# y through memory in rows by channel, and the tail one batch ahead inside the up projections

## The reference, cut to what matters

```python
# x: (4, 512, 256); 32 heads of width 8, state 64; everything in fp32
sa, ca, ga, sb, cb, gb = modulation(c)                      # per batch, per channel
h = layernorm(x) * (1 + ca) + sa
proj = h @ W_in.T                                           # xBC | z | A_log
xBC = causal_conv4(xBC) + conv_b                            # per channel, 4 taps
xh, Bm, Cm = split(xBC)                                     # (l, 32, 8), (l, 32, 64), (l, 32, 64)
a = -softplus(A_log);  Lm = exp(segsum(a))                  # lower triangle of decays, per head
M = einsum('blhn,bshn,bhls->bhls', Cm, Bm, Lm)
y = einsum('bhls,bshp->blhp', M, xh) + D * xh
x = x + ga * (y * silu(z + z_bias) @ W_out.T)
h = layernorm(x) * (1 + cb) + sb
x = x + gb * (fwht(silu(h @ W1.T) * (h @ W3.T)) @ W2.T)     # hidden width 1024
```

## Time and profile before

| | |
|---|---|
| median of 3 runs | 618.3 us |
| the profiled execution's own time | 619.35 us |
| its span | 617.5 us |
| PE busy | 591.9 us, 96% |
| DVE busy | 474.5 us, 77% |
| ACT busy | 382.0 us, 62% |
| POOL busy | 222.9 us, 36% |
| chain that ended last | PE 89%, DVE 7%, issue 2%, ACT 1%, POOL 1% |
| DMA | 51.75 MB, mean 84 GB/s |

### The profile page before, as it was taken

One profiled execution on the slowest core, in us unless ns is written; L12 is line 12 of the kernel. 1 busy time (PEld: TensorE's weight loads), 2 busy tenths in 40 slices (PEclk: granted clock), 3 DMA queues, 4 the chain that ended last, 5 costly groups with the idle time before them and its releaser, 6 DMA issues.

```text
span 617.5 us, 18850 instructions
## 1 busy us (share of the span) xinstructions
PE 591.9 (96%) x6890; PEld 488.6 (79%) x6890; DVE 474.5 (77%) x794; ACT 382.0 (62%) x953; POOL 222.9 (36%) x435
## 2 busy tenths in 40 slices
PE   3898999999999999999999999999969999999997
PEld 3787777877878887887887887887858898888987
DVE  4883989999999999989989989989575564455353
ACT  0665778778778868868868878877523404314240
POOL 2560257455455455346356356586010010000000
PEclk9997999999999999999999999999999999999999
DMA  8400533333332332342342342532020010010101
GB/s 295 196 0 4 194 130 102 102 110 97 96 114 89 98 119 85 100 121 80 100 126 74 99 133 69 170 100 76 32 68 1 0 55 15 0 34 1 35 0 35
DMA packets 29286, 51.75 MB, mean 84 GB/s; under 512 B 3268, under 2 KB 10052, under 8 KB 29000
## 3 DMA queue, kind: packets, MB, share of 16 engines
q1 hardware_dynamic: 29256, 51.34, 26.1%
HBM read 48.97 MB, written 2.37 MB: 83 GB/s over the span
## 4 chain that ended last, share of the span: by engine, by line
PE 89%; DVE 7%; issue 2%; ACT 1%; POOL 1%; DMA 0%; SPq 0%; DVEq 0%
PE ps L250 19%; PE ps L251 17%; PE ps L252 17%; PE ps L390 10%; PE ps L433 5%; PE ps L409 4%; PE ps L373 4%; PE ps L424 4%; PE ps L551 2%; PE ps L443 2%; DVE acc L889 2%; DVE acc L961 1%; DVE xn L867 1%; PE ps L261 1%; PE ps L453 1%
## 5 line engine op out<-in xcount | busy, mean ns | idle before, releaser
L961 DVE SCALAR_TENSOR_TENSOR acc<-ps,cw_dve,acc 128x510 f32<-128x510 f32 (+2 forms) x384 | 264.1, 740 | 32.6 <-ACT acc L688 31.2
L717 ACT ACTIVATE decay<-sums,p_slot 128x128 f32<-128x128 f32 x512 | 163.0, 394 | 1.1 <-POOL sums L1235 1.1
L1235 POOL TENSOR_SCALAR_AFFINE_SELECT sums<-sums 128x512 f32<-128x512 f32 x128 | 81.1, 635 | 183.3 <-DMA sums<-running_sums 182.7
L688 ACT ACTIVATE acc<-ps,cw_act 128x512 f32<-128x512 f32 x128 | 99.2, 775 | 48.5 <-PE ps L252 48.5
L250 PE MATMUL ps<-ht_hi,wg_hi 128*128 128x512 f32 x256 | 108.4, 424 | 0.0
L251 PE MATMUL ps<-ht_lo,wg_hi 128*128 128x512 f32 x256 | 101.7, 397 | 0.0
L252 PE MATMUL ps<-ht_hi,wg_lo 128*128 128x512 f32 x256 | 101.6, 397 | 0.0
L949 DVE TENSOR_TENSOR mix<-ps,decay 128x1024 f32<-128x1024 f32 x64 | 77.7, 1215 | 2.7 <-PE ps L390 2.7
L390 PE MATMUL ps<-acc 64*64 64x64 f32 (+1 forms) x2048 | 69.8, 255 | 1.0 <-DVE mix L949 1.0
L815 ACT ACTIVATE silu_sb<-ps 128x512 f32<-128x512 f32 x32 | 19.1, 598 | 72.4 <-PE ps L252 72.4
L390 PEld LDWEIGHTS ps<-acc 64*64 64x64 f32 x2048 | 54.4, 132 | 12.0 <-issue 12.0
(11 more groups left out here) (137 smaller groups left out, 975.7 us busy)
## 6 DMA issues: line engine op xcount, KB each, us to landing
sums<-running_sums SPq DMA_DIRECT2D x128, 256.0 KB, 3.2
wg_raw<-in_w_bc SPq DMA_DIRECT2D x8, 512.0 KB, 4.6
u_sb<-in_u SPq DMA_DIRECT2D x4, 512.0 KB, 8.2
stage<-in_w SPq DMA_DIRECT2D x1, 2048.0 KB, 12.2
u<-in_u SPq DMA_DIRECT2D x4, 512.0 KB, 3.4
out<-x_tok SPq DMA_DIRECT2D x3, 512.0 KB, 2.9
wmod_sb<-in_wmod SPq DMA_DIRECT2D x1, 1024.0 KB, 8.5
gates<-gate_rows SPq DMA_DIRECT2D x4, 256.0 KB, 3.5
```

Source lines behind the costliest of these rows:

```text
L688: af(acc[:, b % 2, t, :], ps[:, PROJ_BANK[t], :], ACT.Identity, bias=cw_act[:, t, 1:2], scale=cw_act[:, t, 0:1]).then_inc(s[f"tap_a{t}"], 1)
L717: i = af(decay[:, j, c * P:(c + 1) * P], sums[:, j, c * P:(c + 1) * P], ACT.Exp, scale=-1.0, bias=p_slot[:, b * CH + c, j:j + 1])
L961: stt(a[:, d:], ps[:, PROJ_BANK[t], 0:L - d], cw_dve[:, t, TAPS - 1 - d:TAPS - d], a[:, d:], ALU.mult, ALU.add).then_inc(s[f"taps{t}"], 1)
L1235: gp.affine_select(out=v, in_=v, compare_op=ALU.is_ge, fill=FAR, base=0, pattern=[[0, CH], [1, P]], channel_multiplier=-1).then_inc(s["mas ...
```

## The change

What it does:

- The y transposes of the head loop, the scaling by decays and the addition of D x in it, and the transposes of y in the tail are gone. ScalarE copies y of a unit (two buffers), and SyncE stores it to memory, by channel. The convolved x is stored by channel at the start, and so are the decay rows exp(-sum).
- For each batch of the tail SyncE loads (`load_front`) the inner y, the earlier y, the decay rows and x, all by channel, in 8 transfers. GpSimd combines y from its two parts (`y_sum`), VectorE adds D x and multiplies by silu(z) (`gate`).
- The order of a head step is new on every engine; scores of head pair 1 move into the next step, ahead of the other projections. Tiles are taken in the order 1, 0, 3, 2.
- In the tail the front of batch b+1 is inside the up projections of batch b: z projection ahead of tile 2, output projection ahead of tile 4, and on VectorE gate, residual, statistics and normalisation ahead of the products of tiles 3, 5, 6 and 7. The tail is written out for each batch instead of looped.

The diff, cut to its core:

```diff
+ORDER = (1, 0, 3, 2)
+PLACE = [ORDER.index(t) for t in range(GT)]
...
 # SyncE
+            for b in range(B):
+                for t in range(KT):
+                    n = KT * b + t
+                    sp.wait_ge(s["xtaps"], 3 * (n + 1))
+                    sp.dma_start(x_d[n * P:(n + 1) * P, :], acc[:, n // GT, n % GT, :]).then_inc(s[f"st_x{n // GT}"], 16)
...
+            def store_y(g, b):
+                sp.wait_ge(s["yt_ev"], g * B + b + 1)
+                sp.dma_start(y_d[bass.ds((b * NG + g) * P, P), :], yt_sb[:, b % 2, :]).then_inc(s["st_y"], 16)
+            def step(g, b, gr):
+                for j in range(3):
+                    load_sum(g, b, j)
+                if gr is not None:
+                    store_y(gr, (b - 2) % B)
+                load_sum(g, b, 3)
+            def load_front(b):
+                for kt in range(KT):
+                    own = y_d[(b * NG + 4 * kt) * P:(b * NG + 4 * kt + 4) * P, :].rearrange("(q r) l -> q r l", r=QD)
+                    load(yi[:, kt, :], own[:, 0:HD, :], "ld_front")
+                    load(yo[:, kt, :], own[:, HD:2 * HD, :], "ld_front")
+                    rows = e_d[b * NH + 16 * kt:b * NH + 16 * (kt + 1), :].unsqueeze(1).to_broadcast([16, HD, L])
+                    load(ee[:, kt, :], rows, "ld_front")
+                    load(xt[:, kt, :], x_d[(KT * b + kt) * P:(KT * b + kt + 1) * P, :], "ld_front")
...
+            sp.wait_ge(s["bfly"], 6)
+            sp.wait_ge(s["st_e"], 16 * CH)
+            sp.wait_ge(s["w_split"], NG * 2 * GT)
+            load_front(0)
+            store_y(NG - 1, B - 2)
+            sp.wait_ge(s["proj2"], NG * B)
+            load(u2[:], u_b[0], "ld_res")
+            store_y(NG - 1, B - 1)
+            sp.wait_ge(s["st_y"], 16 * NG * B)
+            for b in range(1, B):
+                sp.wait_ge(s["oproj"], 2 * b)
+                load_front(b)
+                sp.wait_ge(s["x1_done"], 2 * b)
                 load(u2[:], u_b[b], "ld_res")
...
 # TensorE
-                    pe.wait_ge(s["w_split"], (g * GT + t) * 2 + 2)
+                    pe.wait_ge(s["w_split"], (g * GT + PLACE[t]) * 2 + 2)
...
             def step(g, b, gq, gr):
+                proj(g, b, 1)
                 if r is not None:
                     states(r, br)
-                    proj(g, b, 0)
-                    proj(g, b, 1)
+                    scores(r, br, 1, False)
+                b_transposes(q, bq, 0, first)
+                proj(g, b, 0)
+                proj(g, b, 3)
+                proj(g, b, 2)
                 if r is not None:
                     inter(r, br, isinstance(r, int) and r == 0)
                     intra(r, br)
-                b_transposes(q, bq, 0, first)
                 scores(q, bq, 0, first)
-                    proj(g, b, 2)
-                    proj(g, b, 3)
                 b_transposes(q, bq, 1, first)
-                if r is not None:
-                    y_transposes(r)
-                scores(q, bq, 1, first)
...
+                    if b + 1 < B:                      # in up(b), per tile m
+                        if m == 2:
+                            z_project(b + 1, 4)
+                        if m == 4:
+                            pe.wait_ge(s["h32b_done"], KT * (b + 1))
+                            out_project(b + 1, 6)
...
+            z_project(0, 0)
+            states(q, B - 2)
+            scores(q, B - 2, 1, False)
+            b_transposes(last, B - 1, 0, False)
+            inter(q, B - 2, False)
+            intra(q, B - 2)
+            pe.wait_ge(s["bfly"], 6)
+            w2_transform(0)
+            w2_transform(1)
+            scores(last, B - 1, 0, False)
+            b_transposes(last, B - 1, 1, False)
+            out_project(0, 0)
+            scores(last, B - 1, 1, False)
+            states(last, B - 1)
+            w2_transform(2)
+            w2_transform(3)
+            inter(last, B - 1, False)
+            intra(last, B - 1)
+            norm2_transposes(0)
+            for b in range(B):
+                up(b)
+                down(b, 0)
+                down(b, 1)
+                if b + 1 < B:
                     norm2_transposes(b + 1)
                 down(b, 2)
                 down(b, 3)
...
 # ScalarE
             def last_tap(g, b, t):
+                if not (isinstance(n, int) and n < 2):
+                    if t == 1:
+                        act.wait_ge(s["score"], 8 * (n - 1))
+                    elif t:
+                        act.wait_ge(s["intra"], JH * (n - 1))
...
                 if r is not None:
                     state_copies(r)
                 decays(q, bq, 0, first)
                 decays(q, bq, 1, first)
+                last_tap(g, b, 1)
+                last_tap(g, b, 0)
+                decays(q, bq, 2, first)
+                b_evacuate(q, 0)
+                last_tap(g, b, 3)
+                last_tap(g, b, 2)
                 if r is not None:
+                    y_evacuate(r, b % 2, early=(isinstance(r, int) and r < 2))
+                b_evacuate(q, 1)
                 decays(q, bq, 3, first)
...
 # VectorE
+                tap(g, b, 1, 0)
                 tap(g, b, 0, 0)
+                tap(g, b, 1, 1)
                 tap(g, b, 0, 1)
+                tap(g, b, 1, 2)
+                tap(g, b, 0, 2)
                 mix_pair(q, 0, first)
+                tap(g, b, 3, 0)
                 tap(g, b, 2, 0)
+                tap(g, b, 3, 1)
                 tap(g, b, 2, 1)
+                tap(g, b, 3, 2)
                 mix_pair(q, 1, first)
                 tap(g, b, 2, 2)
...
             def gate(b):
+                dve.wait_ge(s["ysum"], b + 1)
                 for kt in range(KT):
+                    stt(yi[:, kt, :], xt[:, kt, :], d_ch[:, kt:kt + 1], yi[:, kt, :], ALU.mult,
+                        ALU.add).then_inc(s["y_x"], 1)
+                for kt in range(KT):
+                    dve.wait_ge(s["y_x"], KT * b + kt + 1)
                     dve.wait_ge(s["silu_z"], KT * b + kt + 1)
+                    tt(yi[:, kt, :], yi[:, kt, :], sz[:, kt, :], ALU.mult).then_inc(s["gated"], 1)
...
+                    if b + 1 < B:                      # in hidden(b), ahead of tile m
+                        if m == 3:
+                            gate(b + 1)
+                        if m == 5:
+                            residual1(b + 1)
+                        if m == 6:
+                            statistics2(b + 1)
+                        if m == 7:
+                            normalise2(b + 1)
...
+            w2_lower(0)
+            w2_lower(1)
+            mix_pair(last, 0, False)
+            gate(0)
+            residual1(0)
+            mix_pair(last, 1, False)
+            statistics2(0)
+            w2_lower(2)
+            w2_lower(3)
+            normalise2(0)
+            h2_low(0)
...
 # GpSimd
+                mask(n, 0)
                 if split:
                     await_unit("ld_wg", (g + 2) * 16)
+                    split_after(g, b, 1)
+                mask(n, 1)
+                if split:
                     split_after(g, b, 0)
                 scale_by_decays(g, n, b, early)
+                mask(n, 2)
                 own_x(g, n, b, early)
                 mask(n, 3)
                 if split:
+                    split_after(g, b, 3)
                     split_after(g, b, 2)
...
+            def y_sum(b):
+                pool.wait_ge(s["ld_front"], 16 * 8 * (b + 1))
+                for kt in range(KT):
+                    gp.tensor_tensor(yo[:, kt, :], yo[:, kt, :], ee[:, kt, :], ALU.mult).then_inc(s["y_scaled"], 1)
+                for kt in range(KT):
+                    pool.wait_ge(s["y_scaled"], KT * b + kt + 1)
+                    i = gp.tensor_tensor(yi[:, kt, :], yi[:, kt, :], yo[:, kt, :], ALU.add)
+                i.then_inc(s["ysum"], 1)
+            for b in range(B):
+                y_sum(b)
                 inverse_root(b, "eps2", "rs2")
```

More of the change, by code:

```diff
@@ L371, in b_transposes @@
                     pe.wait_ge(s["bt_ev"], 2 * q + p)
+                if not first and p == 0:
+                    pe.wait_ge(s["st_copy"], 2 * q)
                 for c in range(CH - 1):
@@ L588, in down @@
                 i.then_inc(s["down_mm"], 1)
-            def ffn_step(b, normed, ahead):
-                up(b, b + 2 if normed else B)
-                if normed:
-                    norm2_transposes(b + 1)
-                if ahead:
-                    z_project(b + 2, 0)
-                    z_project(b + 2, 1)
-                down(b, 0)
-                if ahead:
-                    yT_transposes(b + 2, 2)
-                down(b, 1)
-                if ahead:
-                    out_project(b + 2, 2)
+            last, q = NG * B - 1, NG * B - 2
@@ L790, in _ @@
                     step(g, b, gq=(g - 1 if b == 0 else g), gr=(g - 1 if b < 2 else g))
-            step(None, 0, gq=NG - 1, gr=NG - 1)
+            last, r = NG * B - 1, NG * B - 2
             def silu_gate(b):
@@ L813, in hidden @@
```

(5 more changed lines are left out.)

434 lines of the change are left out of this document (140 added, 294 removed).

## The result

The changed kernel takes **667.6 us** (median of 4, 665.8 to 667.8) against 618.1 us before (median of 4 on the same chip): ratio 1.079, 95% interval 1.077 to 1.081. The forecast was 638 us in a range of 618 to 656. The sign was right, and the time is 29.6 us above it. The profiled execution took 667.57 us, with a span of 665.8 us and a mean granted clock of 0.949.

What follows compares the result with a forecast made beforehand. TensorE, busy 54.00 of 54.00 us in the head loop, was taken as the bound. Span: 617.5 - 17.3 - 4.3 + 3.4 + 16.1 + 7.7 + 1.6 + 1.1 + 10.2 + 1.2 = 637.2, adjusted to 638 us; range 618 to 656.

Steps and rivals of the forecast that it cites:

- What TensorE no longer does: Head loop and tail: y transposes go, -17.3 and -4.3 us; rearranged steps of 11.3 us give back +3.4 us.
- The group boundary: Every fourth head step, 7 times: TensorE waits 2.3 us for GpSimd's split of tile 3, +16.1 us.
- The front of batch 0: Ahead of the first output projection: uncovered hole of 7.7 us for loads (7.5 us for eight), sum and gate.
- Inside the up projections: Tail, three batches: holes of 2.0 us at the output projection and 1.8 us at down(b, 0), +10.2 us net.
- The contention: Tail: normalisation on VectorE slowed beside GpSimd's sum of y, +1.2 us for two batches.
- The clock: TensorE's granted clock falls once, behind the hole ahead of the first output projection, +1.6 us.
- the clock falls at each wait: Rival, chance 0.13: TensorE's clock falls behind each hole, thirteen times 1.6 us, giving 659 us.
- The beginning: Start of the kernel: new stores and small loads on SyncE, ends -1 and +2 us, taken as 0.

Runs made afterwards that it cites:

- Experiment 2: Changed kernel with GpSimd's split of tiles 3 and 2 moved ahead of the fourth mask: 643.3 us.
- experiment 3: Changed kernel with GpSimd's sum of y for batches 1 to 3 waiting for the previous batch's normalisation: 661.8 us.
- experiment 4: Changed kernel with eight overwritten matmuls on TensorE ahead of the third tile's weight wait at each of seven group boundaries: 664.2 us.
- experiment 7: Kernel of experiment 2 with tail output projections one tile later, normalisation behind the last remainder, and GpSimd's sums waiting for the normalisation before: 618.5 us.
- experiment 8: Kernel of experiment 2 with overwritten matmuls put into TensorE's holes of the tail: 635.6 us.
- Experiment 5: Kernel of experiment 2 with the decay rows in their own buffer and without ScalarE's wait for their stores: 639.7 us.
- experiment 1: Changed kernel with the decay rows in their own buffer and without ScalarE's wait for their stores: 662.4 us.

## Why the prediction was too low

**What TensorE no longer does.** Right in sign, and worth more than forecast. The step was taken at 11.3 us with 11.19 as the lower bound and is 11.12. Three transposes behind the scores cost 0.31 us (260.77 to 261.08), less than the 0.48 of the earlier trace rows: the bound took the dear place of a neighbour for granted. In the loop that is -18.3 us for a forecast of -13.9.

**The group boundary.** Right: 16.1 forecast, 17.5 measured, with the place and the releaser as named. The walk on the earlier trace rows can be checked link by link on the timelines after (ScalarE's fourth decays; GpSimd's mask, cast and `wg_lo`; TensorE's third tile):

```profile
344.08 1.29 ACT L725 ACTIVATE decay<-sums,p_slot 128x128 f32<-128x128 f32 x4
...
348.86 0.63 POOL L1190 TENSOR_SCALAR_AFFINE_SELECT sums<-sums 128x512 f32<-128x512 f32 x1 [3.87 <-DMA sums<-running_sums]
349.44 0.40 POOL L1138 CAST wg_hi<-wg_raw 128x256 fp32r<-128x256 f32 x1
350.03 0.72 POOL L1140 TENSOR_TENSOR wg_lo<-wg_raw,wg_hi 128x256 fp32r<-128x256 f32 x1 [0.19 <-POOL wg_hi L1138]
...
350.81 0.50 PE L296 MATMUL ps<-ht_hi,wg_hi 128*128 128x512 f32 x1 [2.46 <-POOL wg_lo L1140]
```

Experiment 2 removes it by moving one call.

**The front of batch 0.** Right in kind: a hole without cover, 11.06 us for 7.7. The mis-sized link is the load: 7.5 us was taken from four transfers that landed in 3.5 us each, and it took 11.5 us (441.86 to the landing before 453.37). SyncE's timeline has some 0.6 us for each issue where 0.44 was taken, and the last of the eight landed 7.0 us after its issue:

```profile
441.86 1.23 SPq L167 DMA_DIRECT2D stage<-y_parts  x2
443.13 0.60 SPq L167 DMA_DIRECT2D ee<-decay_rows  x1
443.77 0.59 SPq L167 DMA_DIRECT2D xt<-x_channels  x1
```

**Inside the up projections.** The output projections' holes are right (1.91 for 2.0). Those ahead of `down(b, 0)` are not: 4.8, 4.8 and 1.2 us for 1.8 each. The third, with no sum on GpSimd, is what the queue of products makes, 1.2 us for 1.8. The other 3.6 us of the first two are contention.

**The contention.** The term was 1.2 us, from the earlier trace rows, where four normalisations lost 0.62 us beside one GpSimd copy. Beside GpSimd's four operations of the sum they take 5.13 us for 1.38, twice. Measured by the third hole it is some 7 us, of which experiment 3 took back 4.1. The row was of another kind of operation: one copy that overlapped only a part of the normalisation. The rule of the Trainium skill in *SBUF — State Buffer*, section *Who interferes with whom*, that the two engines take turns a whole instruction long, would have given up to 8 us by the prediction's estimate, and the trace agrees with it: the normalisation ends at 517.0, with GpSimd's four operations (516.8).

**The clock: the step that failed.** "A hole of 7.7 us, which is long enough for the clock to fall: +1.6 us" was the only fall in the sum, and holes of 2 to 2.3 us were taken for free because one of 1.62 had been. Granted clock 0.50, that is 1.2 GHz, came in the changed kernel behind three of seven holes of 2.3 to 2.7 us, two of three of 1.91 and both of 4.8. The price is 6.4 us in the loop (experiment 2; 6.0 by experiment 4), 9 us from up(0) on (experiments 7 and 8, two ways), and 2.1 us between the z projection of batch 0 and up(0) (experiment 8): some 17.5 us for 1.6. The rival *the clock falls at each wait* had this at 659 us and 0.13. It should have been the forecast: between a hole of 1.62 us that kept the clock and one of 3.12 that lost it, the forecast's holes lay in the middle, and the side that costs nothing was taken for all thirteen. Of the 28.6 us of excess the clock is 15.9, the beginning 5.7, the holes ahead of `down` 4.3, the longer hole of batch 0's front 3.4 and the boundaries 1.4, less 4.4 for the shorter steps: 26.3. The rest is not assigned.

**The beginning.** Taken as 0 with ends of -1 and +2; it was +5.7. Of this 1.6 us stand before ScalarE's wait (VectorE's first taps behind the modulation at 63.48 for 61.90), with the granted clock below 1.00 from 48 to 60 us in both traces but lower in the changed one; the kernel of experiment 2, which is the same there, has them at 62.07, so this part is not shown to come from the change. For the rest, the prediction asked only what the stores of decay rows delay on SyncE. It missed that ScalarE waits for their landing, because the rows lie in a buffer that the first mix overwrites, with VectorE and TensorE behind ScalarE. Experiment 5 prices it at about 4 us, the 5.7 less the 1.6.

## What to carry to other kernels

Price each new hole on TensorE twice: as the wait, and as the chance that the clock falls behind it, from the nearest rows on both sides. Here a hole of 2 to 2.5 us cost about 2 us more in half of the cases, so thirteen small holes were a large term and filling or removing them was worth more than their length. When a buffer gets a new store, list every engine that must wait for the store to land, not only the queue that issues it. Two engines that slow each other down still do so when one is moved by a few microseconds: look at what it then stands beside (experiment 3). And ask of each moved call what is now queued ahead of it: moving `mask`, `normalise2` and `out_project` by one place each, with GpSimd's sums held back behind the normalisation, turned this change from 7.9% slower to equal, and the rest to 1.8% faster.

## What the runs showed of the hardware

- The same hole does not always cost the clock: in the changed kernel's trace 2.3 to 2.7 us kept 1.00 at four boundaries and lost it at three, and the profiled execution of experiment 1, with the same holes, lost it at five. That kernel's four executions differ by 8.4 us (659.3 to 667.7, mean granted clock 0.961 to 0.949), where seven of the kernel before, run beside them, stay within 5.0 (617.8 to 622.9).
- How long it stays at the lower level differs too: in the first steps the granted clock is 0.53 and 0.61 in 76 to 84 us in experiment 2, while in experiment 8 it is below 1.00 until 92 us, which costs 2.7 us more in the same code.
- Matmuls that compute nothing, put into holes, kept the granted clock at 1.00 (experiments 4 and 8). In a hole of 11.4 us 42 of them took no time: from the z projection of batch 0 to the first output projection it is 22.4 us with and without them. In holes of 2.3 to 2.7 us eight of them made each wait some 0.2 us longer.
- Beside GpSimd's sum of y VectorE's operations took longer: four normalisations 5.13 us for 1.38 (the changed kernel), two remainders 3.13 for 1.46 (experiment 3).
